# Computing the derived weights of layers 1 to 3 during the last convolution of layer 0

## The reference, cut to what matters

```python
x = x + _L0_conv_ref(_gn(x), ...)   # gated recurrence over the pixels, a 3x3 convolution (conv2_w), then
                                    # batch normalization (bn_g, bn_b) over ALL 16 images, leaky relu
x = x + _L1_conv_ref(_gn(x), ...)   # six-qubit circuit per token and head, softmax attention
x = x + _L2_conv_ref(_gn(x), ...)   # deformable 3x3 depthwise convolution
x = x + _L3_conv_ref(_gn(x), ...)   # expand to 510, 2x2 FFT filter, depthwise 3x3, gelu gate, project
```

```python
for d in range(Q_DEPTH):
    for i in range(N_QUBITS):
        state = _apply_1q(state, _rx(w[d, i, 0]), i)
        state = _apply_1q(state, _ry(w[d, i, 1]), i)
        state = _apply_1q(state, _rz(w[d, i, 2]), i)
    for i in range(N_QUBITS):
        state = _cnot(state, i, (i + 1) % N_QUBITS)
```

## Time and profile before

| | us |
|---|---|
| median of 3 runs (8632.81 to 8636.24) | 8635.48 |
| the profiled execution's own time | 8692.87 |
| its span, first to last instruction | 8691.1 |
| mean granted TensorE clock, share of full | 0.936 |
| last image's convolution on PE | 3076.5 to 3108.9 |
| first instruction of `dve_add` (L1851) | 3193.2 |

### The profile page before, as it was taken

One profiled execution on the slowest core, in us unless ns is written; L12 is line 12 of the kernel. 1 busy time (PEld: TensorE's weight loads), 2 busy tenths in 40 slices (PEclk: granted clock), 3 DMA queues, 4 the chain that ended last, 5 costly groups with the idle time before them and its releaser, 6 DMA issues.

```text
span 8691.1 us, 101545 instructions
## 1 busy us (share of the span) xinstructions
PE 7786.5 (90%) x37966; PEld 3888.1 (45%) x37966; DVE 5733.4 (66%) x9725; ACT 3843.5 (44%) x7430; POOL 2195.4 (25%) x1798
## 2 busy tenths in 40 slices
PE   7999999999999957698898899999999899999877
PEld 4555555555555532243344344344344344344343
DVE  4676666776676634576676676676676676676664
ACT  4555555555555514334344344344435335434320
POOL 1122222222222200124134134134124134124152
PEclk9999999999999977799999999999999999999988
DMA  1111111111111120144454444454444444444365
GB/s 65 37 37 41 44 53 43 43 37 37 42 48 48 42 74 4 65 133 154 112 138 150 116 137 154 113 139 155 116 133 155 115 135 155 124 126 155 104 196 137
DMA packets 244235, 850.13 MB, mean 98 GB/s; under 512 B 46412, under 2 KB 49176, under 8 KB 243360
## 3 DMA queue, kind: packets, MB, share of 16 engines
q1 hardware_dynamic: 150272, 388.71, 16.6%
q0 software_dynamic: 92160, 453.06, 16.4%
q10 hardware_dynamic: 1312, 1.87, 0.1%
HBM read 602.10 MB, written 89.68 MB: 80 GB/s over the span
## 4 chain that ended last, share of the span: by engine, by line
PE 43%; DVE 14%; issue 4%; ACT 4%; DMA 2%; POOL 1%; SPq 0%; another core or an unknown queue 0%; DVEq 0%; ACTq 0%; POOLq 0%
PE ps L2241 9%; DVE arena L1931 5%; PE ps L2693 5%; PE ps L2474 4%; PE ps L389 4%; PE ps L2230 4%; PE ps L2672 3%; PE ps L2704 2%; PE ps L2163 2%; PE ps L2147 2%; PE ps L2358 2%; DMA arena<-img,arena 1%; PE ps L2190 1%; PE ps L2206 1%; PE ps L2456 1%
## 5 line engine op out<-in xcount | busy, mean ns | idle before, releaser
L2507 POOL DMA_INDIRECT arena<-img,arena x1152 | 1398.2, 1214 | 2766.2 <-DMA img<-arena 1762.9
L2402 DVE SCALAR_TENSOR_TENSOR arena<-arena 128x384 f32<-128x384 f32 x1152 | 747.1, 649 | 581.3 <-DMA arena<-img,arena 539.1
L1931 DVE TENSOR_REDUCE arena<-ps 128x2 f32<-128x1024 f32 x768 | 894.2, 1216 | 332.6 <-PE ps L2206 329.8
L2086 ACT ACTIVATE arena<-ps 128x512 f32<-128x512 f32 x1536 | 829.6, 599 | 498.8 <-PE ps L2230 328.8
L2241 PE MATMUL ps<-arena 128*64 128x512 f32 x3072 | 906.8, 675 | 0.0
L998 POOL TENSOR_TENSOR arena<-arena 128x512 f32<-128x512 f32 x384 | 443.1, 1161 | 1755.7 <-DMA arena<-decay 1755.3
L2693 PE MATMUL ps<-arena 128*64 128x512 f32 x3072 | 793.1, 638 | 72.3 <-ACT arena L2651 38.2
L2474 PEld LDWEIGHTS ps<-arena 128*96 128x96 f32 x4608 | 525.1, 165 | 210.8 <-issue 206.6
L389 PE MATMUL ps<-arena 128*128 128x256 f32 x2432 | 596.2, 396 | 9.9 <-DVE arena L1783 8.6
L2474 PE MATMUL ps<-arena 128*96 128x128 f32 x4608 | 576.3, 279 | 26.2 <-DVE arena L2391 25.3
L2230 PE MATMUL ps<-arena 32*128 32x512 bf16 x1536 | 407.7, 410 | 181.3 <-issue 131.2
(11 more groups left out here) (349 smaller groups left out, 12435.4 us busy)
## 6 DMA issues: line engine op xcount, KB each, us to landing
arena<-arena SPq DMA_DIRECT2D x1024, 144.5 KB
arena<-decay SPq DMA_DIRECT2D x384, 256.0 KB, 3.2
img<-arena SPq DMA_DIRECT2D x162, 384.0 KB, 2.6
arena<-img,arena POOLq DMA_INDIRECT x1152
arena<-y SPq DMA_DIRECT2D x16, 768.0 KB, 6.5
arena<-x SPq DMA_DIRECT2D x16, 768.0 KB
out<-arena SPq DMA_DIRECT2D x16, 768.0 KB
arena<-x SPq DMA_DIRECT2D x16, 512.0 KB, 5.1
```

The lines of the kernel that those rows point to most:

```text
L1931: dve.tensor_reduce(out, self.wides[B.at("max", b, g, n, h) // 2].rearrange("p (a b) -> p a b", a=2), AX.X, AL.max).then_inc(*S.mark("max_ ...
L2086: act.activation(self.p[n % 6], B("score", b, n)[:, :], ACT.Exp).then_inc(*S.mark("p_act", b, n))
L2402: dve.scalar_tensor_tensor(gb[:, 0:384], gb[:, 384:768], pp[:, 1, n:n + 1], gb[:, 0:384], AL.mult, AL.add).then_inc(*S.mark("corner_x", b, n))
L2507: pool.indirect_dma_start(self.g[n % 6], None, img, bass.IndirectOffsetOnAxis(ap=ii[:, n:n + 1], axis=0)).then_inc(*S.landed(f"{self.tag}g ...
```

## The change

`Layer0.stages` takes a further generator, `prepare`, and draws it together with the last convolution: 21 steps of `conv`, 28 of `prepare`. All five methods of `Prepare` became generators with `skip`s that set where their parts fall. They wait for the last join's result on DVE (`joined`) in place of the normalization's shift. The two chains of rounds run abreast, with one of the eight `WF` products between (`spectrum`). The small products stand before the rounds. The angles' and tau's ACT work stands ahead of the convolution's L1429. `Prepare` uses layer 0's PSUM banks. Its tiles and those of layers 2 and 3 move to offset 26280, its temporary ones to 44980, clear of what the convolution reads. `sp_fetch` of image 0 no longer waits for `prepared`, nor SP for the zeroed images until layer 2 first writes one. ACT and POOL wait for the last store of `y` before they write over its source.

```diff
@@ Layer0.stages
-        run(conv(NB - 1))
+        weave((conv(NB - 1), 21), (prepare, 28))
@@ Prepare.sp
-        sp.wait_ge(*S("bn_dve", "shift"))
-        sp.wait_ge(*S("bn_dve", "shift"))
+        yield
+        sp.wait_ge(*S(*self.joined))
         sp.dma_start(self.wt, dram["WB"]).then_inc(*S.landed("wb", 0))
...
+        yield
         sp.wait_ge(*S("zero", "image"))
@@ Prepare.pool
-        pool.wait_ge(*S("bn_dve", "shift"))
+        yield
+        pool.wait_ge(*S(*self.joined))
+        pool.wait_ge(*S("parts", self.joined[1], "last"))
@@ Prepare.pe
+        yield from skip(16)
         pe.wait_ge(*S("wb", 2))
...
+        yield from abreast(circ(0), circ(1))
@@ Prepare.dve
+        yield
         dve.wait_ge(*S("wb", 2))
...
+        yield from skip(2)
         dve.wait_ge(*S("prep_act", "sin", 1))
...
+        yield from skip(13)
         dve.wait_ge(*S("zero", "weights"))
...
+        def spectrum():
+            yield
+            dve.wait_ge(*S("ws"))
+            for k in range(2):
+                for q in range(4):
+                    dve.scalar_tensor_tensor(self.WF[:, k, 510 * q:510 * q + 510], self.TW["WIN"][:, k, :], 0.25, self.TW["FW"][:, q, :], AL.mult, AL.mult)
+                    yield
+
+        pair = abreast(circ(0), circ(1), spectrum())
...
+        dve.memset(self.tb, 0.0).then_inc(*S.mark("prepared"))
@@ build
+        keep, once = Arena(arena, 26280), Arena(arena, 44980)
+        P = Prepare(S, keep, once, L0.B, dram, lay["WB"], lay["CB"], lay["CO"], lay["WS"], ("join_dve", NB - 1, "y", 2))
...
+        ar = keep
@@ sp_program
-            P.sp(sp)
-            sp.wait_ge(*S("img_zero", 1, PW * PW // 128 * 128))
-            sp.wait_ge(*S("prepared"))
             L1.sp_fetch(sp, 0)
```

More of the change, by code:

```diff
@@ L1455, in sp_conv, with stages @@
             sp.dma_start(dst[128:192, H(h)], self.yo[64 * h:64 * h + 64, 2, :]).then_inc(*S.landed(f"y_out{b % 2}", b, h))
-    def stages(self, NB, ahead, enter, project, chunks, norm, join, conv):
+    def stages(self, NB, ahead, enter, project, chunks, norm, join, conv, prepare):
         def scan(b):
@@ L1651, in pe, with circ @@
         S, B, W, C = self.S, self.B, self.W, self.C
+        yield from skip(16)
         pe.wait_ge(*S("wb", 2))
-        for s in range(2):
+        for s, nm in ((0, "JQ"), (1, "JK")):
+            ps, free = B.take(("pc", s), ("prep", "small", "pc", s))
+            pe.wait_ge(*free)
+            pe.matmul(ps[0:6, 0:4], W[nm], C["C4"], start=True, stop=True).then_inc(*S.mark("prep_pe", "small", "pc", s))
+        for n, (m, v) in enumerate((("C48", "JB"), ("C36", "PB"))):
+            ps, free = B.take(("b", n), ("prep", "small", "b", n))
+            pe.wait_ge(*free)
+            pe.matmul(ps[0:128, 0:1], C[m], W[v], start=True, stop=True).then_inc(*S.mark("prep_pe", "small", "b", n))
+        yield
+        for s in range(2):
+            ps, free = B.take(("zt", s), ("prep", "small", "zt", s))
+            pe.wait_ge(*free)
+            pe.wait_ge(*S("prep", "small", "pc", s))
+            pe.matmul(ps[0:128, 0:4], C["QZ"], self.pc[s], start=True, stop=True).then_inc(*S.mark("prep_pe", "small", "zt", s))
+        ps, free = B.take(("pp",), ("prep", "small", "pp"))
+        pe.wait_ge(*free)
+        pe.matmul(ps[0:96, 0:6], W["PRE"], C["C6"], start=True, stop=True).then_inc(*S.mark("prep_pe", "small", "pp"))
+        yield
+        def circ(s):
             for n, cd in enumerate((3 + 2 * s, 2 + 2 * s, 1, 0)):
@@ L1696, in dve @@
             dve.tensor_tensor(dst, dst, rd, AL.subtract).then_inc(*S.mark("prep", "trig", n))
+        dve.scalar_tensor_tensor(ta, W["RT"], -1.0, W["RT"], AL.mult, AL.min).then_inc(*S.mark("prep", "tau", 0))
+        dve.scalar_tensor_tensor(tb, C["SV"][:, 0:1], 2.0, C["SV"][:, 1:2], AL.mult, AL.add)
+        yield from skip(2)
         dve.wait_ge(*S("prep_act", "sin", 1))
@@ L1736, in dve, with circ @@
             n *= 2
+        yield from skip(13)
         dve.wait_ge(*S("zero", "weights"))
         for s in range(2):
+            dve.wait_ge(*S("prep_pe", "small", "pc", s))
+            dve.tensor_copy(self.pc[s], B("pc", s)[0:6, 0:4]).then_inc(*S.mark("prep", "small", "pc", s))
+        for n, dst in enumerate((self.B48, self.B36)):
+            dve.wait_ge(*S("prep_pe", "small", "b", n))
+            dve.tensor_copy(dst, B("b", n)[0:128, 0:1]).then_inc(*S.mark("prep", "small", "b", n))
+        dve.wait_ge(*S("prep", "small", "b", 1))
+        dve.tensor_tensor(self.B36, self.B36, C["E1"], AL.add)
+        dve.wait_ge(*S("prep_act", "ln"))
+        after(dve.scalar_tensor_tensor(ta, W["RT"], 0.0, ta, AL.max, AL.add), "tau", 1)
+        after(dve.reciprocal(ta, ta), "tau", 2)
+        dve.tensor_tensor(sv[:, 0:1], tb, ta, AL.mult)
+        dve.scalar_tensor_tensor(sv[:, 1:2], C["SV"][:, 6:7], ta, C["SV"][:, 5:6], AL.mult, AL.add)
+        yield
+        def circ(s):
             ra, rn = self.ra[s], self.rn[s]
@@ L1754, in dve @@
                     i.then_inc(*S.mark("prep", "circ_in", s, 4))
+        def spectrum():
+            yield
+            dve.wait_ge(*S("ws"))
+            for k in range(2):
+                for q in range(4):
+                    dve.scalar_tensor_tensor(self.WF[:, k, 510 * q:510 * q + 510], self.TW["WIN"][:, k, :], 0.25, self.TW["FW"][:, q, :], AL.mult, AL.mult)
+                    yield
+        pair = abreast(circ(0), circ(1), spectrum())
+        next(pair)
         for s in range(2):
-            dve.wait_ge(*S("prep_pe", "small", "pc", s))
-            dve.tensor_copy(self.pc[s], B("pc", s)[0:6, 0:4]).then_inc(*S.mark("prep", "small", "pc", s))
             dve.wait_ge(*S("prep_pe", "small", "zt", s))
@@ L2769, in build @@
         L2z = Layer2(S, over, over, P, L1.B, dram, "z")
-        assert over.at <= ar.at, (over.at, ar.at)
+        assert over.at <= ar.at <= 26280, (over.at, ar.at)
+        ar = keep
         own = Arena(arena, ar.at)
@@ L2811, in both, with stored @@
             run(three(last))
+        def stored(engine):
+            engine.wait_ge(*S(f"y_top{last % 2}", last))
+            engine.wait_ge(*S(f"y_out{last % 2}", last, 1))
         def pe_program(eng):
@@ L2861, in pool_program @@
             pool = Pool(eng)
-            L0.pool(pool, NB)
-            P.pool(pool)
-            pool.wait_ge(*S("img_zero", 1, PW * PW // 128 * 128))
+            L0.pool(pool, NB, P.pool(pool))
+            stored(pool)
+            pool.wait_ge(*S("zero", "image"))
+            pool.wait_ge(*S("bn_dve", "shift"))
             L1.pool_setup(pool)
```

79 lines of the change are left out of this document (25 added, 54 removed).

## The result

The changed kernel takes **8564.11 us** (median of four runs, 8550.92 to 8573.43), the kernel before, measured beside it, 8635.86 (8632.81 to 8646.29): a ratio of 0.9912, 95% interval 0.9899 to 0.9925, 71.8 us less. That interval stands for 65 to 87 us. Forecast were 52.1 us less and 8583.4, in a range that began at 8576.

The account below looks back on a forecast made before the run. Bound: 84.3 us between layer 0's last convolution on PE and layer 1's first addition, a chain of waits. That shrinks to 14.2, the convolution grows by 18, saving 52.1: 8635.48 - 52.1 = 8583.4 us, range 8576 to 8598.

Parts of the forecast that it names:

- The loads, the angles, the long row: Prepare at the border: weights on DVE 10.7 us after the release, angles 1.8, long row 14.7, ending at 3099.5.
- The price of the table load: ACT's table load in the angles: 1.28 us by the trace; the skill's figure would end the long row 1.4 earlier.
- PE's stalls: PE waits twice for DVE in the last convolution of layer 0: 1.6 us, then 2.2 us.
- The second stall: PE waiting for DVE's round copy until 3109.0, before the first L1690: 2.2 us.
- DVE until the rounds: DVE's small copies, sums and first round operands behind the first move-out to 3104.5, through the second move-out to 3108.7.
- The clock: PE's clock in the woven stretch: about one dip, 2 us, convolution ending at 3126.9, 18.0 us later than before.
- Rival A: The lower clock stays through the woven stretch: PE ends at 3138.5, saving 40.5 us, time 8595; chance 0.18.
- After the convolution: From the convolution's end on PE to layer 1's first addition: 14.2 us, with the load of `x` ending last.
- Rival B: Weights arrive late, `CO` waiting until all 24 transfers are through at about 3100: saving 35 us, time 8600; chance 0.04.
- The rest: Layers 1 to 3 moved as a whole, other edits cost nothing: 5498 us from the addition to the end as before.
- Rival C: Border gain given back, or weave worse on DVE: saving 17 to 35 us, chance 0.04; under 17, 0.03.
- D: Moved tiles of layers 2 and 3 slow their instructions: break-even 45 ns each, 8699 us at 100 ns; chance 0.03.

Follow-up runs that it names:

- e1_placement: The kernel before with only the tiles moved to the change's addresses, order and waits as before: 8677.3 us, ratio 1.001 to the kernel before.
- e3_after_again: The changed kernel run again, unaltered: 8611.46 us, ratio 0.992 to the kernel before.
- e10: The changed kernel without layer 2's gathers from the third image on: 8345.85 us, the kernel before in that series 8680.12.
- e11: The changed kernel with plain copies of the same bytes for layer 2's gathers from the third image on: 8380.15 us, one run, kernel before 8680.12.

## Why the forecast was right in part and wrong in its number

**The loads, the angles, the long row: right.** DVE started 10.7 us behind the release (3094.15 - 3083.45), the row ended at 3110.67, which less 11.15 is 3099.5, the forecast to 0.1. The price of the table load came from the row (1.28). With the drain that the Trainium skill adds (page "ScalarE: Activation LUTs", section "What ACT_TABLE_LOAD costs"), the row would have ended 1.4 us earlier than it did. The trace speaks for the smaller price: from the first angle instruction to the row it took 1.78 us (3095.93 - 3094.15), forecast 1.8.

**PE's stalls: the first right, the second too large.** 1.97 us for a forecast 1.6, then the first round at 3114.48 - 11.15 = 3103.3 for a forecast 3104.5. The second stall, forecast at 2.2 us before the first L1690, doesn't exist: those matmuls start at 3119.24 with no wait, right behind the block. *DVE until the rounds* was sized too long.

**The clock: a dip, but cheaper.** It was at 0.67 on average over 3110 to 3120, around the wait of 1.97 us. One block of the convolution ran in it (8 matmuls in 1.97 us where later ones take 1.08), and then it was at 0.99 to the end. By the rule of the Trainium skill on pauses between groups that go through PSUM banks in turn (page "TensorE: Matmul & The Clock Gate", section "A second HAM failure mode: psum-queue depth-cycling") the clock would have swung between its levels; it fell once, so this trace doesn't bear it out. Rival A is out. The first L1690 came at 3108.1 for a forecast 3109.0. From it to the last block it took 14.6 us, and forecast were 14.8, 1 of waits and 2 for the clock; the dip lay nearly all ahead of it. Together the convolution ends on PE at 3133.79 - 11.15 = 3122.6, **13.8 us later than before in place of 18.0**. These 4.2 us are all of the border's surplus. There is some luck in them: three of the twelve traced executions lost 3 us more to the clock.

**After the convolution: right.** 14.26 us from PE's end to the addition, forecast 14.2, and `x` is what is waited for. The first half of ACT's pass ends 1.5 us earlier, so the table load saved there is worth nothing, as forecast. Rival B is out too: `CO` was there after 9.79 us.

**The step that failed** is *The rest. Layers 1 to 3 have the same lists, so they are moved as a whole*. The lists are the same, and DVE's costliest group of layer 2 takes as long (649 ns before, 644 after), but the time isn't: 5421 and 5507 us in two executions of one program in the first two series, 5203 in the last. The forecast took its start from three runs within 3.4 us of each other and gave the rest no spread, though the profiled execution, 57.4 us above their median, spoke for one. With the border as measured the same sum gives 8635.48 - 56.3 = 8579.2, inside the range. Of the 71.8 us, 56.3 are the border. That the remaining 15.5 are what this rest does from run to run fits the other series (55.4 to 61.3 us), but isn't shown for this one, whose own interval of 65 to 87 us leaves the border's 56.3 out. Against a gain of these layers by the change itself stand e1_placement, whose rest is that of before, and e3_after_again, whose rest is longer than that of before. Rival C would have saved 35 us or less in the border. By my estimate from these spreads the range had to be wider by some 20 us to both sides, even with every term of the border right. One sum on the range was off as well: half of C, all of D and B make 0.105, not 0.14.

**What is shown and what is open.** Shown: a shorter Prepare (32.7 us) and its place beside the convolution (23.4) make the border's gain, and the kernel's gain is of that size whether the kernel before takes 8668 or 8415 us. Shown too, for the series in which the kernel before takes 8614 to 8728: the indirect gathers beside the attention bring PE's pauses and the low clock, whatever their bytes. This rests on e10 and above all on e11, where both cases lie in one execution. The changed kernel itself wasn't run in their series. Open: by which way the gathers do it, and why in two series the same gathers do no harm. The records give one chip number to a series at 8668 and to one at 8417, so that number doesn't decide it. No complete kernel here is faster than the changed one by more than the spread of its runs.

## What to carry to other kernels

Cut both executions at the same two instructions and compare the pieces: what a change does shows in its own piece (here to 0.6 us in nine executions of twelve, 3 us off in the others), and what the other pieces do from run to run is the least width that a range of the whole can have. A few runs close together don't measure that spread; look for it in the trace, as a stretch that repeats in a loop and is never of the same length. And when a path of dependent work is laid beside another stage, run it once more in its old place with all other edits kept: here more than half of the border's gain was a shorter path (32.7 of 56 us, 19 of them in the rounds and products), and less than half the new place.

## What the runs showed of the hardware

The unexpected part is the price of indirect transfers beside a tight exchange between PE and ACT. With a gather every 1.3 us on POOL, exponentials started 2.53 and 5.21 us into ACT's idle time though the matmuls ahead of them were over by the record, PE was busy 6.7 of 18 us, and its clock fell to 0.50 and stayed there for 3 to 27 us; plain copies of the same 384 KB, at about the same rate (290 to 326 GB/s against 273 to 308), did none of this. With them the rest took 5421 to 5507 us, without them 5213 to 5224. It comes and goes with the series: the same program, gathers and all, ran its layers 1 to 3 in 5507 and in 5203 us.
